# A graph network and expert stack on one core: the transposed adjacency mask made by DMAs instead of by TensorE

## The reference, cut to what matters

```python
def _L0_gnn_ref(h, adj, W, b, a):            # N = 2048 nodes, 4 heads of 32
    Wh = (h @ W.T + b).reshape(N, H, D)
    e = leaky_relu(src[:, None, :] + dst[None, :, :], 0.2)
    att = softmax(where(adj[:, :, None] == 1, e, NEG_INF), axis=1)
    return einsum('ijh,jhd->ihd', att, Wh).reshape(N, H * D)

x = x + _L0_gnn_ref(_layernorm(x), adj, ...)
x = x + _L0_ffn_ref(_layernorm(x)[None], ...)[0]   # 8 experts of 512, the best 2 weighted
x = x + _L1_gnn_ref(_layernorm(x), adj, ...)       # one attention matrix from the mean over heads
x = x + _L1_ffn_ref(_layernorm(x)[None], ...)[0]   # two layers, 16 experts by route_id, one shared
```

## Time and profile before

| | |
|---|---|
| Time, median of 3 runs (lowest to highest) | 630.83 us (628.54 to 633.81) |
| Profiled execution: its time, its span | 632.04 us, 630.3 us |
| Mean granted TensorE clock | 0.941 of full speed |
| Busy: TensorE, weight load | 542.1 us (86%), 429.6 us (68%) |
| Busy: VectorE, ScalarE, GpSimd | 516.3 us (82%), 372.2 us (59%), 178.9 us (28%) |
| Chain that ended last, by engine | TensorE 46%, VectorE 31%, ScalarE 10%, issue 5%, GpSimd 3%, DMA 2% |

### The profile page before, as it was taken

The page is one execution under the profiler, slowest core; times in us unless marked ns, Lnnn a source line. Parts: engine busy times, 40 slices in busy tenths (PEclk is TensorE's granted clock), DMA queues, the critical chain, the costliest instruction groups (busy, mean ns, idle before and its releaser), DMA issues.

```text
span 630.3 us, 13281 instructions
## 1 busy us (share of the span) xinstructions
PE 542.1 (86%) x5082; PEld 429.6 (68%) x5082; DVE 516.3 (82%) x907; ACT 372.2 (59%) x756; POOL 178.9 (28%) x186
## 2 busy tenths in 40 slices
PE   1979777999999999799998897999996855899985
PEld 1768674978866877667686565578886645567753
DVE  6799999997797756899849728999999899999630
ACT  1699795768885787586755745542331401566473
POOL 3311000165311201984522010021315000364941
PEclk9989896989998999899998899899999688799999
DMA  6485930022245346999598215020201844476750
GB/s 141 88 166 109 260 83 1 18 86 85 89 133 197 107 133 219 221 212 237 110 209 97 68 23 180 2 68 0 68 1 42 298 144 141 121 224 190 211 178 18
DMA packets 48857, 78.36 MB, mean 124 GB/s; under 512 B 5406, under 2 KB 24870, under 8 KB 48794
## 3 DMA queue, kind: packets, MB, share of 16 engines
q1 hardware_dynamic: 30714, 52.02, 26.2%
q0 software_dynamic: 15488, 22.02, 20.5%
q10 hardware_dynamic: 2592, 3.48, 1.9%
HBM read 80.61 MB, written 22.06 MB: 163 GB/s over the span
## 4 chain that ended last, share of the span: by engine, by line
PE 46%; DVE 31%; ACT 10%; issue 5%; POOL 3%; DMA 2%; SPq 1%; ACTq 0%; POOLq 0%; DVEq 0%
DVE arena L1641 17%; PE bank L698 13%; PE bank L710 10%; PE bank L627 10%; PE bank L867 4%; ACT arena L1143 3%; DVE arena L1464 3%; ACT ysb L1095 2%; POOL x L550 2%; DVE arena L1468 1%; PE bank L824 1%; DMA routed_sums<-in_wsT 1%; PE bank L603 1%; PE bank L576 1%; PE bank L808 1%
## 5 line engine op out<-in xcount | busy, mean ns | idle before, releaser
L483 POOL TENSOR_TENSOR x<-x,ysb 128x512 f32<-128x512 f32 x36 | 75.9, 2107 | 245.5 <-ACT ysb L1095 233.5
L1143 ACT ACTIVATE arena<-heads,nd 128x512 bf16<-128x512 f32 x176 | 111.8, 720 | 21.4 <-PE bank L627 21.0
L698 PE MATMUL bank<-hTc,arena 128*128 128x512 f32 x192 | 95.9, 656 | 5.6 <-ACT reg_c L1084 5.6
L1641 DVE SCALAR_TENSOR_TENSOR arena<-reg_b,nd,arena 128x1536 f32<-128x1536 f32 x48 | 92.0, 1977 | 0.0
L710 PEld LDWEIGHTS bank<-arena,reg_c 128*128 128x128 f32 x768 | 87.6, 192 | 4.8 <-issue 4.7
L710 PE MATMUL bank<-arena,reg_c 128*128 128x128 f32 x768 | 88.5, 276 | 0.0
L1084 ACT ACTIVATE reg_c<-bank,b 128x512 f32<-128x512 f32 x96 | 65.3, 687 | 25.8 <-PE bank L698 25.7
L627 PEld LDWEIGHTS bank<-reg_b,arena 128*128 128x128 bf16 x1536 | 73.4, 99 | 7.0 <-DVE arena L1497 4.0
L627 PE MATMUL bank<-reg_b,arena 128*128 128x99 bf16 x1536 | 74.6, 211 | 3.8 <-DVE arena L1497 3.8
L1095 ACT ACTIVATE ysb<-bank,comb 128x128 f32<-128x128 f32 x128 | 36.5, 367 | 65.5 <-PE bank L913 39.9
L698 PEld LDWEIGHTS bank<-hTc,arena 128*128 128x128 f32 x192 | 39.2, 211 | 52.7 <-issue 44.3
(11 more groups left out here) (195 smaller groups left out, 844.7 us busy)
## 6 DMA issues: line engine op xcount, KB each, us to landing
maskT<-routed_sums SPq DMA_DIRECT2D x48, 256.0 KB, 3.2
reg_c<-in_adj POOLq DMA_DIRECT2D x16, 512.0 KB, 7.1
arena<-in_w1T SPq DMA_DIRECT2D x16, 512.0 KB, 3.9
arena<-in_w2T SPq DMA_DIRECT2D x16, 512.0 KB, 4.8
routed_sums<-in_wsT SPq DMA_DIRECT2D x32, 256.0 KB, 5.5
routed_sums<-in_wrT POOLq DMA_DIRECT2D x32, 256.0 KB, 12.7
arena<-routed_sums SPq DMA_DIRECT2D x32, 256.0 KB, 3.0
routed_sums<-ident POOLq DMA_DIRECT2D x4, 1024.0 KB, 12.7
```

Source lines behind the costliest of these rows:

```text
L483: nc.gpsimd.tensor_tensor(xi, xi, ysb[:, e % 3, :].rearrange("p (t d) -> p t d", d=P), ALU.add).then_inc(s_acc, 1)
L698: mm(bank[b][:, :], w1[:, s, e % 2, c * P:(c + 1) * P], hTc[:, :], start=True, stop=True).then_inc(full[b], 1)
L1143: last = af(ind[:, q, b, j, :], sbc[:, h, :], ACT.Relu, bias=nd[:, q * QT + j, h:h + 1], scale=BIG)
L1641: last = v.scalar_tensor_tensor(p, row, nd[:, t, h:h + 1], p if h else maskT[:, t, columns], ALU.max, ALU.mult)
```

## The change

What it does:

- GpSimd issues a DMA per row tile that casts `adj` from int32 to bfloat16 into a DRAM tensor `mask_rows` (2048 rows of 2176 elements, 2048 of them used). Tiles 0 to 3 are issued where the loads were; 4 to 7 after the maxima over partitions, each when the transpose four tiles earlier has landed; 8 to 15 each in the loop that adds expert outputs, ahead of an addition.
- SyncE issues a transposing DMA per row tile from `mask_rows` into `maskT`, each when its cast has landed. Tiles 0 to 4 stand ahead of the spill of the source scores, the others between the `load_pair` calls.
- TensorE's 256 transposes and ScalarE's 32 copies are gone, with `identb`, ROWS and the slots in `reg_c`. TensorE and VectorE wait for the four transposes of a chunk (`mask_ready`).
- In chunk 0 ScalarE makes the scaled logits of all four quads of each head, and VectorE takes four minima per head; the eight comparisons are gone. The counts of the semaphores follow.

```diff
+        mask_rows = nc.dram_tensor("mask_rows", (N, N + P), BF16, kind="Internal").ap()
...
+        def mask_ready(engine, c):
+
+            for r in range(CT):
+                engine.wait_ge(s_mask[r], 16 * (c + 1))
...
+            def transpose_rows(rows):
+
+                for r in rows:
+                    sp.wait_ge(s_cast[r % 4], 16 * (r // 4 + 1))
+                    sp.dma_start(maskT[:, :, r * P:(r + 1) * P], mask_rows[r * P:(r + 1) * P, 0:N],
+                                 transpose=True).then_inc(s_mask[r % CT], 16)
+
+            transpose_rows(range(CT + 1))
             sp.wait_ge(ev["score"], 1)
...
             for h in range(H):
+                if h >= 2:
+                    transpose_rows(range(2 * CT + 2 * (h - 2), 2 * CT + 2 * (h - 1)))
                 load_pair(0, h, h >= 2)
+                if h == 0:
+                    transpose_rows(range(CT + 1, CT + 3))
                 if h == 1:
+                    transpose_rows(range(CT + 3, 2 * CT))
                     sp.wait_ge(s_clear, 1)
...
+            transpose_rows(range(3 * CT, T))
             for c in range(1, C):
...
-            def load_rows(r):
-                if r >= 4:
-                    pool.wait_ge(full[5 if r % 2 else 7], (r - 4) // 2 + 1 + (0 if r % 2 else H // 2))
-                pool.dma_start(adj[:, r % 4, :], a["adj"][r * P:(r + 1) * P, :]).then_inc(s_adj[r % 4], 16)
+            def cast_rows(r):
+
+                rows = slice(r * P, (r + 1) * P)
+                if r >= CT:
+
+                    pool.wait_ge(s_mask[r % CT], 16 * (r // CT))
+                pool.dma_start(mask_rows[rows, 0:N], a["adj"][rows, :]).then_inc(s_cast[r % 4], 16)
...
                 pool.wait_ge(ev["y"], n + 1)
+                if n < 2 * CT:
+                    cast_rows(2 * CT + n)
...
-            for r in range(CT):
-                mask_rows(r)
-            pe.wait_ge(ev["mask"], 2 * CT)
+            mask_ready(pe, 0)
             attend_whole(0)
-            mask_rows(CT)
             for h in range(H):
 
                 attend_first(h)
-                for r in ROWS[h][:2]:
-                    mask_rows(r)
...
             for h in range(2):
-                for q in (2, 3):
+                for q in range(Q):
                     above(h, h, q)
-            mask_rows(CT)
-
             act.wait_ge(s_xb, C)
             for h in range(H):
                 head(0, h)
...
+                quads = range(Q) if h < 2 else range(1, 2) if h == 2 else range(2, Q)
+                for q in quads:
+                    above(min(h + 2, H), (h + 2) % H if h < H - 1 else 0, q)
...
-                    if q < 2:
-                        if h >= 2:
-
-                            dve.wait_ge(s_indf, (h - 2) * (Q - 1) + q + 1)
-                        for j in range(QT):
-                            t = q * QT + j
-                            last = v.scalar_tensor_tensor(to[:, j, :], sbc[:, h, :], thr[:, t, h:h + 1],
-                                                          maskT[:, t, 0:CW], ALU.is_gt, ALU.mult)
...
+                    dve.wait_ge(s_above, h * Q + q + 1)
+                    v.tensor_tensor(to, maskT[:, q * QT:(q + 1) * QT, 0:CW], to, ALU.min).then_inc(s_ind, 1)
```

More of the change, by code:

```diff
@@ L228, in gnn_moe_stack @@
         s_w1 = sem("second_mixture_loaded")
-        s_adj = [sem(f"adj_slot{r}_loaded") for r in range(4)]
+        s_cast = [sem(f"mask_rows_mod4_{r}_stored") for r in range(4)]
+        s_mask = [sem(f"mask_rows_mod4_{r}_transposed") for r in range(CT)]
         s_spill = sem("later_source_scores_stored")
@@ L282, in gnn_moe_stack @@
         NW1 = 4
[L283 to L285 removed]
+        NC = 7
         HB = (2, 3, 6, 7)
         HT = (5, 6, 7)
[L288 to L289 removed]
+        BANK3 = C + (C - 1) * E0 + 1
+        BANK5 = (C - 1) * (E0 // 2 + 1) + len(range(0, E0 * HC, len(HT))) + C
         FFN_Y = C * (E0 + 1)
@@ L342, in load_pair @@
                 if wait:
-                    sp.wait_ge(full[5], T // 2 + c * (H + 1) + (h if h >= 2 else h - 1))
+                    sp.wait_ge(full[5], c * (H + 1) + (h if h >= 2 else h - 1))
                 e = slice(2 * h, 2 * h + 2)
@@ L456, in _ @@
             nc.gpsimd.partition_all_reduce(gmax[:, :], pmax[:, :], P, RMAX).then_inc(s_gm, 1)
-            for r in range(4, T):
-                load_rows(r)
+            for r in range(CT, 2 * CT):
+                cast_rows(r)
             k = Count()
@@ L581, in normalised @@
                 pe.wait_ge(ev["hTc"], k.at("hTc"))
-            def mask_rows(r):
-                pe.wait_ge(s_adj[r % 4], 16 * (r // 4 + 1))
-                for half in range(2):
-                    b = MASK_BANKS[r % 2][half]
-                    use(b, "mask")
-                    for j in range(T // 2):
-                        jt = half * T // 2 + j
-                        last = nc.tensor.transpose(bankb[b][:, j * P:(j + 1) * P],
-                                                   adj[:, r % 4, jt * P:(jt + 1) * P], identb[:, :])
-                    last.then_inc(full[b], 1)
             def project(s, c, banks=(2, 3)):
@@ L755, in _ @@
                     last.then_inc(full[4], 1)
-                for r in ROWS[h][2:]:
-                    mask_rows(r)
             def chunk0(c):
@@ L1006, in ln_out @@
                    ACT.Copy).then_inc(ev["hTc"], 1)
-            def mask_rows(r):
-                for half in range(2):
-                    b = MASK_BANKS[r % 2][half]
-                    got(b)
-                    af(maskT[:, half * 8:(half + 1) * 8, r * P:(r + 1) * P],
-                       bankb[b].rearrange("p (j i) -> p j i", i=P), ACT.Copy).then_inc(ev["mask"], 1)
             def project(whx, c, banks=(2, 3)):
@@ L1169, in _ @@
                 head(0, h)
-                if h == 2:
-                    act.wait_ge(s_u, H)
-                rows = list(ROWS[h])
-                if h == H - 1:
-                    above(H, 0, 3)
-                quads = ((2, 3), (2, 3), (1, 2), ())[h]
-                for j in range(3):
-                    if h == 0 and j == 2:
-                        got(4)
-                        for c in range(1, C):
-                            part = slice((c - 1) * GRP, (c - 1) * GRP + H)
-                            last = af(hTc[part, :], bank[4][part, :], ACT.Copy)
-                        last.then_inc(ev["score"], 1)
-                    for q in quads[j:j + 1]:
-                        above(h + 2, (h + 2) % H, q)
-                    for r in rows[j:j + 1]:
-                        mask_rows(r)
+                quads = range(Q) if h < 2 else range(1, 2) if h == 2 else range(2, Q)
+                for q in quads:
+                    above(min(h + 2, H), (h + 2) % H if h < H - 1 else 0, q)
+                if h == 0:
+                    got(4)
+                    for c in range(1, C):
+                        part = slice((c - 1) * GRP, (c - 1) * GRP + H)
+                        last = af(hTc[part, :], bank[4][part, :], ACT.Copy)
+                    last.then_inc(ev["score"], 1)
             act.wait_ge(s_w2, 16 * NW2)
@@ L1524, in _ @@
             dve.wait_ge(ev["rows"], H)
-            dve.wait_ge(ev["mask"], 2 * CT)
+            mask_ready(dve, 0)
             def score_bounds():
@@ L1608, in _ @@
                 norm(c - 1, c - 1 + C)
-                dve.wait_ge(ev["mask"], c * 2 * CT + 2 * CT)
+                mask_ready(dve, c)
                 indicate(c, 0, range(2))
```

24 lines of the change are left out of this document (6 added, 18 removed).

## The result

| | before | changed |
|---|---|---|
| Median of 4 runs on one chip (lowest to highest) | 631.66 us (628.54 to 633.81) | 643.58 us (641.7 to 645.62) |
| Profiled execution: its time, its span | 632.04, 630.3 us | 642.31, 640.5 us |
| Mean granted TensorE clock | 0.941 | 0.923 |
| Busy: TensorE, VectorE, ScalarE | 542.1, 516.3, 372.2 us | 527.8, 504.3, 362.5 us |

The changed kernel took 1.0193 times as long, 95% interval 1.0135 to 1.0251; on another chip, later, 1.0124 (1.0042 to 1.0207). Three engines have 10 to 14 us less to do, and it is 12 us slower.

The account below looks back on a forecast made before the run. VectorE bounds the kernel from 38.56 to 97.61 us, then TensorE, also at chunk 2. -3.2 + 9.6 + 1.0 = +7.4 us on 632.04 gives 639.4, 638.2 at the median, so 638 us; range 628 to 654.

Parts of the forecast that it names:

- the forecast case: Masks in time at the start, weights late at chunk 2: 638 us, own range 633 to 650; chance 0.60.
- rival B: Slow transposes delay chunk 0's masks and chunk 2's weights: 672 us, at half that price near 645; chance 0.21.
- TensorE waits at chunk 2: Ahead of chunk 2's first expert layer TensorE stands 9.6 us for a weight pair behind tile 15's cast and transpose.
- rival D: At chunk 2 cast and transpose finish within the cover, the weight pair is not late: 627.5 us; chance 0.07.
- The masks are hidden: At the start, chunk 0's last transposed mask tile lands at 27 to 32 us; VectorE wants it at 38.6.
- the upper row of 12.7 us: Upper bound for a DMA transpose: the slowest kind in the old trace, an accumulating 256 KB transfer, 12.7 us.
- The gain of 3.2 us in chunk 0: Chunk 0's ScalarE copies end at 85.9 instead of 89.07 us; gain 4.8 us if TensorE stays at full clock.
- VectorE's saving doesn't come through: In chunk 0 VectorE saves 12.4 us on paper; 9 us of it turn into waiting for ScalarE's order.
- rival C: In chunk 0 VectorE's saving comes through whole: 629 us, 624 with the weight wait at its lower bound; chance 0.12.
- The third and fourth weight pairs: Chunk 0's third and fourth pairs are issued about 7 us later, where some 22 us are spare: harmless.
- The issues of casts during VectorE's minima: GpSimd's cast issues might be blocked while VectorE runs minima: an estimated 2.5 us more wait, not added to the sum.
- The clock, +1 us: After the stop at chunk 2 TensorE's clock starts low: 1 us added, range 0 to 2.

Follow-up runs that it names:

- Experiment 1: Changed kernel with transposes 12 to 15 behind chunk 1's second weight pair, not ahead of the first: 634.3 us, 1.0020 of before.
- experiment 2: Changed kernel with casts 4 to 7 held until transposes 0 to 3 have landed: 640.73 us, 1.0137 of before.
- experiment 6: Changed kernel with late transposes 12 to 15 and held casts 4 to 7: 629.83 us, 0.9985; with chunk 0's old VectorE/ScalarE sharing too: 634.47 us, 1.0032.
- experiment 3: Changed kernel with chunk 0's old sharing (VectorE compares quads 0, 1; ScalarE makes 2, 3), masks still by DMA: 645.94 us, 1.0213.
- Experiment 4: Changed kernel with head 2's whole sums copied by ScalarE after two quads of head 3, not four: 640.24 us, 1.0111 of before.
- experiment 5: Changed kernel, casts 4 to 15 once chunk 0's transposes landed, transposes 4 to 8 before the spill, others in chunk 0: 647.53 us, 1.0255.

## Why the prediction was right, and where its steps were off

The time, 643.6 us, lies in the range and 5.6 us above the value named; the forecast case happened where its largest term lies, and one step of it did not. By the number alone rival B's half-price line, "near 645 us", is closer, but its weight wait of 15 us did not come.

- **TensorE waits at chunk 2: right, mechanism and size.** 8.2 us against 9.6, in the sum 187.8 + 4.9 + 2.4 + 0.6 + 5.1 and 0.1 of gaps = 200.9 against 200.1. Four terms were off and cancel, and that they do is luck. The cast took 4.9 us, not 6.5: no more than the load into SBUF took. The transpose held SyncE for 2.4 us, not 0.5. The weight pair's second load took 5.1 us, not 7.3. And the output that cast 15 waits for came 2.4 us later, since the program was 2.2 us behind. Experiment 1 took the wait away and with it nearly all of the slowdown; rival D is out.
- **The masks are hidden: wrong.** This is the step that failed. Instead of 27 to 32 us the last one is there at 41.3 us. "At 3 to 4 us each after the casts" had two errors. A transpose is not issued in 0.5 us; the first three held SyncE for 12.2 us together. That alone cost little: without casts 4 to 6 beside them the masks were there at 33.1 us (experiment 2). The large error is that those casts, which the change itself puts there, were left out: beside them the fourth transpose took 13.3 us, near the upper row of 12.7 us, without them 4.9. Rival B's half-price line, "end at 41 us" and "2 us late", is what chunk 0 did, for a reason B did not have.
- **The gain of 3.2 us in chunk 0: right in mechanism, and did not come.** Its size hung on the step above. ScalarE's order stood as worked through, late by 4 us throughout: head 0's sums copied at 53.3 against 49.3 us, head 3's quads begun at 68.2 against 64.5, head 2's whole sums copied at 78.5 against 74.8. The slow TensorE behind it was there: 5.5 and 5.9 us against 4.6 and 5.64. So the scores came 1.5 us late (0.1 in experiment 1's execution) instead of 3.2 early. With the masks on time and this order they came 1.8 us before 97.61 in experiment 2 (95.84) and 4.1 us in experiment 6 (93.56), where the clock stayed up at head 3; the forecast of 3.2 lies between these two.
- **VectorE's saving doesn't come through (against rival C): right.** 12.4 us on VectorE were worth 0.8 to 2.2 us at the scores as the change stands (experiment 3) and 3.2 to 5.5 us with the masks on time (experiment 6). Experiment 4 supports the reason given: with the copy moved ahead of two of the four quads, the scores come 3.9 to 5.3 us earlier. No run moves the copy under the old sharing, so how much of the held-back saving this one place accounts for is not shown.
- **The third and fourth weight pairs: harmless, as forecast.** They were issued at 142.3 and 156.8 us, 15.7 and 8.9 us later than before and not about 7: the casts that stand ahead of them landed only at 140.1 and 154.0 us. Nothing waits for the pairs.
- **The issues of casts during VectorE's minima: no sign of harm.** They took 0.52 to 0.89 us each; the forecast rightly added nothing for this, and the 2.5 us of its estimate were not seen.
- **The clock, +1 us: open.** The first layer behind the wait took 8.56 us here, against 8.81 before; behind the same wait it took 8.59, 10.12 and 10.20 us in experiments 3, 2 and 4, so between nothing and 1.4 us. The mean granted clock fell from 0.941 to 0.923, and where the low stretches fall differs between executions, so the spans don't settle this term.

The sum: +7.4 us predicted, about +12 measured by the medians and +8 to +12 by the two ratios. The profiled spans differ by 10.2 us, which can be followed: +1.5 to the scores of chunk 0 (forecast -3.2), +0.7 from there to the scores of chunk 2 (no term), +8.4 to the first layer (forecast +9.6), -0.4 from there to the end (forecast +1). The 4.7 us of chunk 0 are the largest miss, and the two last ones took part of it back.

## What to carry to other kernels

When work moves from engines to DMAs, cost the place in the issuing queue and the other transfers of the same moment as well as the transfer: here the slots of the same casts and transposes alone decided between a ratio of 0.9985 (experiment 6) and 1.0255 (experiment 5). A saving on the engine that holds the chain comes through only as far as the next engine's order lets it; work that order through by hand before making the saving, and move the few copies that others wait for ahead of the bulk. After taking away one wait, measure the other edits again, since their worth can change (0.8 to 2.2 us at the scores became 3.2 to 5.5 here). And look at one mark in more than one execution before reading a difference of 2 us from it: the same order in chunk 0 gave 99.11 and 97.70 us, and 95.84 and 93.56.

## What the runs showed of the hardware

- A transposing DMA of 512 KB held the queue that issues it for microseconds, and for longer beside casting DMAs (20.1 us at the most, in experiment 5). All sixteen in the changed kernel (duration in ns min/median/max), and the time to landing of all mask DMAs:

```profile
L343 SPq DMA_TRANSPOSE maskT<-mask_rows x16: 1898/3256/9022, 15.6 to 192.8; - x16
...
DMA to landing us min/median/max: 4.4/6.5/13.3
```

  An ordinary weight DMA of the same bytes occupied SyncE for 0.4 to 0.6 us (195.20 and 195.82 us). The Trainium skill ("Advanced Engine Details and Errata", X-Bar Transpose) has transposing DMAs as fast as regular ones; from issue to landing that holds here when no cast is beside it (4.9 us for the fourth in experiment 2, 5.1 us for the weight load), and neither for the time in the issuing queue nor beside casting DMAs (13.3 us). The 1.3 to 1.5 us for 512 KB, the prediction's estimate from the page's rate, was not seen; the shortest took 4.4 us to land.
- Small packets: the change adds 33,280 packets under 512 bytes (38686 against 5406), some 2,080 for each of 16 transposes.
- TensorE's granted clock in the window from 92 to 96 us, at the start of work, was 0.62 and 0.50 after pauses of 3.6 and 9.3 us, and 1.00 without a pause. The same 16 products took 9.2 us after either pause and 7.1 us without.
